# Four cross-attention layers on one core: the last wide job trades places with the first narrow job of layer 4

## What is computed

```
narrow (layers 0 and 3): xn = x * rsqrt(mean(x*x) + eps) * norm_w
    q = xn @ wq (16 heads of 8), k, v = cond @ wk, cond @ wv (4 key heads, shared by 4)
    x = x + softmax(q k^T / sqrt(8)) v @ wo
wide (layers 1 and 2): q = x @ Wq (16 heads of 64), k, v = ctx @ Wk, ctx @ Wv
    x = x + softmax(q k^T / 8 + col_bias) v @ Wo + bo
```

## Time and profile before

| | us |
|---|---|
| median of 3 runs | 382.94 |
| the runs | 382.94, 382.5, 452.04 |
| the profiled execution, its time | 384.65 |
| the profiled execution, its span | 382.9 |
| PE busy in the span | 359.0 |
| DVE busy | 268.5 |
| ACT busy | 278.9 |
| POOL busy | 187.4 |

### The profile page before, as it was taken

One profiled execution on the slowest core, in us unless ns is written; L12 is line 12 of the kernel. 1 busy time (PEld: TensorE's weight loads), 2 busy tenths in 40 slices (PEclk: granted clock), 3 DMA queues, 4 the chain that ended last, 5 costly groups with the idle time before them and its releaser, 6 DMA issues.

```text
span 382.9 us, 10493 instructions
## 1 busy us (share of the span) xinstructions
PE 359.0 (94%) x3522; PEld 319.2 (83%) x3522; DVE 268.5 (70%) x1401; ACT 278.9 (73%) x1176; POOL 187.4 (49%) x220
## 2 busy tenths in 40 slices
PE   6799899999999999999999999999999999978655
PEld 6698698899989998989889988888999889867444
DVE  0999985564654566696888886667465775699982
ACT  3687998875575585657798999997666865647891
POOL 1576964552332245446576765443333435447661
PEclk9789999999999999999999999999999999999998
DMA  7915000000000000000000000000000000000000
GB/s 229 409 57 221 0 3 3 2 3 0 3 2 2 1 2 3 2 1 2 3 9 9 7 10 2 3 3 2 0 3 2 3 2 1 2 3 3 7 7 15
DMA packets 4739, 9.91 MB, mean 26 GB/s; under 512 B 592, under 2 KB 3024, under 8 KB 4432
## 3 DMA queue, kind: packets, MB, share of 16 engines
q1 hardware_dynamic: 4400, 8.99, 6.7%
q10 hardware_dynamic: 288, 0.27, 0.2%
HBM read 8.73 MB, written 0.52 MB: 24 GB/s over the span
## 4 chain that ended last, share of the span: by engine, by line
PE 74%; DVE 17%; ACT 5%; DMA 1%; issue 1%; SPq 0%; DVEq 0%
PE pt_ps L844 12%; PE scores_ps L831 9%; PE v_ps L895 8%; PE fill_ps L696 8%; PE q_ps L791 8%; PE v_ps L877 7%; PE fill_ps L697 7%; PE fill_ps L698 7%; DVE probs L609 7%; ACT probs L478 4%; PE v_ps L865 3%; DVE probsT L620 3%; PE q_ps L783 3%; DVE qn L592 2%; PE scores_ps L820 2%; DVE qn L588 2%
## 5 line engine op out<-in xcount | busy, mean ns | idle before, releaser
L478 ACT ACTIVATE probs<-probs,negmax 128x128 f32<-128x128 f32 x512 | 198.6, 391 | 82.5 <-DVE negmax L609 82.4
L375 POOL TENSOR_TENSOR probs<-probs,inv 128x512 f32<-128x512 f32 x128 | 137.3, 1076 | 178.2 <-DVE inv L616 177.8
L478 ACT ACTIVATION_READ_ACCUMULATOR probs<-probs,negmax 128x1 f32 x512 | 97.0, 190 | 0.0
L609 DVE CUSTOM_DVE_ANT_0 probs<-scores_ps,col_bias 128x128 f32<-128x128 f32 x256 | 58.1, 283 | 39.1 <-PE scores_ps L831 39.1
L844 PE MATMUL pt_ps<-smalls,probs 128*128 128x128 f32 x512 | 69.2, 278 | 7.5 <-DVE probsT L620 7.5
L844 PEld LDWEIGHTS pt_ps<-smalls,probs 128*128 128x128 f32 x512 | 56.6, 142 | 19.1 <-issue 15.8
L609 DVE CUSTOM_DVE_ANT_0 probs<-scores_ps,no_bias,inv_rms 128x128 f32<-128x128 f32 x224 | 64.3, 344 | 6.1 <-PE scores_ps L820 5.7
L620 DVE COPY probsT<-pt_ps 128x512 f32<-128x512 f32 x96 | 62.9, 683 | 2.7 <-PE pt_ps L844 0.6
L609 DVE DVE_READ_ACCUMULATOR2_ANT negmax<- 128x1 f32 x512 | 42.5, 83 | 0.0
L696 PE MATMUL fill_ps<-c_hi,w_hi 128*128 128x256 f32 x128 | 38.5, 301 | 0.0
L831 PE MATMUL scores_ps<-kT,qT 64*128 64x128 f32 x512 | 37.2, 285 | 0.0
(11 more groups left out here) (92 smaller groups left out, 586.0 us busy)
## 6 DMA issues: line engine op xcount, KB each, us to landing
kT<-in_kv_w SPq DMA_DIRECT2D x6, 512.0 KB, 6.9
w_qo<-in_qo_w SPq DMA_DIRECT2D x2, 1024.0 KB, 8.6
v<-in_ctxT SPq DMA_DIRECT2D x4, 256.0 KB, 9.9
v<-in_kv_w SPq DMA_DIRECT2D x2, 512.0 KB, 11.7
outT<-x SPq DMA_DIRECT2D x8, 64.0 KB, 1.6
wn<-in_narrow_w SPq DMA_DIRECT2D x1, 384.0 KB, 6.0
x<-in_xT SPq DMA_DIRECT2D x1, 384.0 KB, 8.5
oT<-in_narrow_kv ACTq DMA_DIRECT2D x1, 256.0 KB, 2.8
```

The source lines that it names most:

```text
L375: nc.gpsimd.tensor_tensor(p4, p4, inv[:, o % 2, side, :].unsqueeze(2).broadcast_to([P, 4, S]), ALU.mult,).then_inc(probs_made[side], 1)
L478: last = nc.scalar.activation(e, e, ACT.Exp, scale=-1.0, bias=negmax[:, o % 2, side, q:q + 1], accum_out=rowsum[:, o % 2, side, q:q + 1])
L609: last = nc.vector.tensor_tensor_reduce(out=probs[:, o % PROBS_RING, side, cols], in0=banks[scores_bank(o)][side][:, cols], in1=bias, scal ...
```

## The change

Two entries of `JOBS` trade places: job 27 becomes (3, 4), narrow, and job 28 becomes (2, 7), wide. The order of the last six jobs is then wide, narrow, wide, narrow, narrow, narrow, where it was wide, wide and four narrow. Layer 3 of items 4 and 7 (jobs 27 and 31) now stands three jobs behind layer 2 of the same item, not four; `is_close` names these two. For them the queries and the mean of squares move to half 2n - 1 on PE, the split to 2n - 1 on DVE, the statistic to the head of half 2n on DVE, and on POOL `square` to 2n - 2 and `inverse_root` to 2n - 1, each between the two normalisations of that half. Three entries of `FILLS` move one or two halves back, and with them the half from which odd scores use `fill_ps` (59, was 57). Buffers of narrow jobs are picked by the index among narrow jobs in place of the parity of n, which gives the same numbers for jobs up to 26.

```diff
+FIRST_LAST, LAST_WIDE = JOBS.index((3, 4)), JOBS.index((2, 7))
+JOBS[FIRST_LAST], JOBS[LAST_WIDE] = JOBS[LAST_WIDE], JOBS[FIRST_LAST]
...
-    50: ["v7.0"], 52: ["v7.1"], 53: ["kn3.3"], 54: ["v7.2"], 55: ["v7.3"],
+    50: ["v7.0"], 52: ["v7.1"], 54: ["kn3.3"], 56: ["v7.2"], 57: ["v7.3"],
...
 def query_half(n):
 
+    if is_close(n):
+        return 2 * n - 1
     return 2 * n - 3 if n >= 2 and is_narrow(n - 1) else 2 * n - 2
 
+def split_half(n):
+
+    return 2 * n - 1 if is_close(n) else query_half(n) + 1
+
+def squares_half(n):
+
+    return 2 * n - 1 if is_close(n) else 2 * n - 2
+
+def is_close(n):
+
+    return is_narrow(n) and JOBS[n][0] > 0 and n - JOBS.index((JOBS[n][0] - 1, JOBS[n][1])) == 3
...
+def place(n):
+
+    return narrow_index(n) % 2
...
-                nc.gpsimd.tensor_tensor(inv_rms[:, n % 2:n % 2 + 1], rms[:, n % 2:n % 2 + 1], half_power[:],
+                nc.gpsimd.tensor_tensor(inv_rms[:, place(n):place(n) + 1], rms[:, place(n):place(n) + 1], half_power[:],
                                         ALU.pow).then_inc(rms_made, 1)
...
             def half(o):
                 if valid(o):
                     normalise(o, 0)
+                for n in NARROW_JOBS:
+                    if o == 2 * n - 2 and is_close(n):
+                        square(n)
+                    if o == 2 * n - 1 and is_close(n):
+                        inverse_root(n)
+                if valid(o):
                     normalise(o, 1)
                 for n in NARROW_JOBS:
-                    if o == 2 * n - 2 and n > 0:
+                    if o == 2 * n - 2 and n > 0 and not is_close(n):
                         inverse_root(n)
-                    if o == 2 * n - 4 and n >= 2:
+                    if o == 2 * n - 4 and n >= 2 and not is_close(n):
                         square(n)
...
-                if h == 1 and is_narrow(n + 1):
-                    mean_out(n + 1)
+                for m in NARROW_JOBS:
+                    if m > 0 and squares_half(m) == o - 1:
+                        mean_out(m)
...
-                    if m > 0 and query_half(m) == o - 1:
+                    if m > 0 and split_half(m) == o:
                         narrow_queries(m)
...
                 if n >= 3:
-                    pe.wait_ge(v_read, uses(n - 3, 1))
-                if n > 0 and is_narrow(n - 1):
-                    pe.wait_ge(rms_out, narrow_index(n - 1) + 1)
+                    pe.wait_ge(v_read, uses(n - 2, 0) if is_close(n) and is_wide(n - 2) else uses(n - 3, 1))
+                if n > 0:
+                    pe.wait_ge(rms_out, narrow_index(n))
...
-                if is_narrow((o + 4) // 2):
+                if is_narrow((o + 4) // 2) and squares_half((o + 4) // 2) < o + 3:
                     pe.wait_ge(rms_out, narrow_index((o + 4) // 2) + 1)
...
+                for m in NARROW_JOBS:
+                    if m > 0 and query_half(m) == o and is_close(m):
+                        queries(m, 0)
                 for name in FILLS.get(o, []):
                     project_context(name)
                 for m in NARROW_JOBS:
-                    if m > 0 and query_half(m) == o:
+                    if m > 0 and query_half(m) == o and not is_close(m):
                         queries(m, 0)
                 if is_wide(n + 1):
                     queries(n + 1, h)
-                if h == 0 and is_narrow(n + 1):
-                    mean_squares(n + 1)
+                for m in NARROW_JOBS:
+                    if m > 0 and squares_half(m) == o:
+                        mean_squares(m)
```

More of the change, by code:

```diff
@@ L349, in narrow_values @@
                     pool.wait_ge(v_full, uses(m, 1))
-                place = v_narrow[:, i % 2].rearrange("p (g s) -> p g s", g=KV_HEADS)[:, :, 0:NARROW_D]
+                blocks = v_narrow[:, i % 2].rearrange("p (g s) -> p g s", g=KV_HEADS)[:, :, 0:NARROW_D]
                 values = vn[:, b, NARROW.index(l)].rearrange("p (g d) -> p g d", g=KV_HEADS)
-                nc.gpsimd.tensor_copy(place, values).then_inc(vn_made, 1)
+                nc.gpsimd.tensor_copy(blocks, values).then_inc(vn_made, 1)
             def inverse_root(n):
                 pool.wait_ge(rms_out, narrow_index(n) + 1)
-                nc.gpsimd.tensor_tensor(inv_rms[:, n % 2:n % 2 + 1], rms[:, n % 2:n % 2 + 1], half_power[:],
+                nc.gpsimd.tensor_tensor(inv_rms[:, place(n):place(n) + 1], rms[:, place(n):place(n) + 1], half_power[:],
                                         ALU.pow).then_inc(rms_made, 1)
@@ L368, in square @@
                     pool.wait_ge(ms_full, narrow_index(n) - 1)
-                nc.gpsimd.tensor_tensor(x_sq[:, n % 2, :], x[:, b, :], x[:, b, :], ALU.mult).then_inc(sq_ready, 1)
+                nc.gpsimd.tensor_tensor(x_sq[:, place(n), :], x[:, b, :], x[:, b, :], ALU.mult).then_inc(sq_ready, 1)
             def normalise(o, side):
@@ L579, in mean_out @@
                 dve.wait_ge(ms_full, narrow_index(n) + 1)
-                nc.vector.tensor_scalar(rms[:, n % 2:n % 2 + 1], ms_ps[:, 0:1], EPS, None, ALU.add
+                nc.vector.tensor_scalar(rms[:, place(n):place(n) + 1], ms_ps[:, 0:1], EPS, None, ALU.add
                                         ).then_inc(rms_out, 1)
@@ L586, in narrow_queries @@
                 dve.wait_ge(q_full, uses(n, 0))
-                all_parts = qn[0:STACK, n % 2].rearrange("p r t -> p (r t)")
+                all_parts = qn[0:STACK, place(n)].rearrange("p r t -> p (r t)")
                 nc.vector.tensor_scalar(all_parts, q_ps[0:STACK, :], -NARROW_SCALE, None, ALU.mult).then_inc(qn_hi_made, 1)
@@ L590, in narrow_queries @@
                 low = slice(PART, 2 * PART)
-                rest = qn[low, n % 2].rearrange("p r t -> p (r t)")
+                rest = qn[low, place(n)].rearrange("p r t -> p (r t)")
                 nc.vector.scalar_tensor_tensor(
@@ L602, in scores_out @@
                 bias = no_bias[:].broadcast_to([P, S]) if l in NARROW else col_bias[:, l - 1, :]
-                scale = inv_rms[:, n % 2:n % 2 + 1] if l in NARROW else 1.0
+                scale = inv_rms[:, place(n):place(n) + 1] if l in NARROW else 1.0
                 if l in NARROW and h == 0 and side == 0:
@@ L798, in mean_squares @@
                 if n >= 3:
-                    pe.wait_ge(v_read, uses(n - 3, 1))
-                if n > 0 and is_narrow(n - 1):
-                    pe.wait_ge(rms_out, narrow_index(n - 1) + 1)
-                nc.tensor.matmul(ms_ps, x_sq[:, n % 2, :], mean_w[:, 0:2], start=True, stop=True).then_inc(ms_full, 1)
+                    pe.wait_ge(v_read, uses(n - 2, 0) if is_close(n) and is_wide(n - 2) else uses(n - 3, 1))
+                if n > 0:
+                    pe.wait_ge(rms_out, narrow_index(n))
+                nc.tensor.matmul(ms_ps, x_sq[:, place(n), :], mean_w[:, 0:2], start=True, stop=True).then_inc(ms_full, 1)
             def scores(n, h):
@@ L819, in scores @@
                     for side in range(2):
-                        nc.tensor.matmul(out[side][:], qn[0:STACK, n % 2, 2 * h + side, :], keys, start=True, stop=True
+                        nc.tensor.matmul(out[side][:], qn[0:STACK, place(n), 2 * h + side, :], keys, start=True, stop=True
                                          ).then_inc(scores_full[side], 1)
```

## The result

The changed kernel takes **389.5 us** (median of 4 runs, 387.75 to 391.06), the kernel before in the same series 382.72 (4 runs). The ratio is 1.0178, with a 95% interval of 1.0114 to 1.0241. One of the four runs before took 452.04 us, a slow one that the ratio leaves out. The median is 3.7 us above the forecast of 385.8 and just above the upper ends of both ranges given with it, 388.6 and 389.2. So it is slower, by 6.8 us in the first series and 4.3 in the second, where 2.9 were forecast.

A forecast was written before the change was run, and what follows sets the result against it. PE was busy 94% of the span, but DVE bound the tail from about 331.86 us. +3.8 us at scores 63, part given back, left +2.9: 382.9 + 2.9 = 385.8 us; own range 383.0 to 388.6, 8 in 10 380.6 to 389.2.

The forecast's parts named there:

- the mechanism of the schedule up to scores 63: Halves 52 to 62: new waits and gaps put DVE's scores 63 at 372.85 against 369.07, +3.8 us.
- DVE's idle time ahead of scores 54 and 62: Halves 54 and 62: DVE idle for some 1.7 us each, put down to the inverse root or its semaphore.
- the term of 1.8: Halves 54 and 62: reciprocal to scores through normalisation and inverse root on POOL, 0.25 + 1.0 + 0.55 us.
- The split wait on PE: Half 53: PE stands still ahead of scores 54 until DVE has split the narrow job's queries, about 1.5 us.
- the gap ahead of `add_input(26)`: Start of half 57: DVE idle 3.25 us, waiting for the output projection at the end of PE's half 56.
- the sum: Delay of DVE's scores 63 from all halves before it, forecast at +3.8 us.
- halves 52 to 54: Work taken off PE pays for both new waits; DVE's scores 55 come at 331.5 against 331.86, 0.35 us left.
- A part is given back: Drain: last transposes follow normalisation directly as the projection ahead ends sooner, cutting the +3.8 to +2.9 us.
- the same chain at the same clock: After the last transposes: the rest of the drain runs as before, so the sum stays +2.9 us.
- rival 2: Tail: standstills drop PE to 1.2 GHz by 360, before projection 28, adding 4.7 us: 390.5 us; chance 0.08.
- Rival 1: Halves 52, 53 and tail: narrow job fills DVE's 3.45 idle us; 380.8 us, at best 379.4; chance 0.22.

The follow-up runs named there:

- e5: Changed kernel with the close jobs' statistic and inverse root made earlier, plus unread constant matmuls in PE's tail standstills: 384.22 us, ratio 1.0011.
- e9: e5 with projection kn3.3 moved to half 53 and v7.2 to half 57, without the added matmuls of those halves: 382.74 us, ratio 0.9983.
- e8: Kernel before, with unread constant matmuls added in PE's standstills of halves 62, 64 and 66: 381.92 us, ratio 0.9952.
- e6: Changed kernel with unread constant matmuls added in PE's standstills from half 53 to 66: 387.34 us, ratio 1.0078.
- e7: Changed kernel, unaltered, measured again in a later series of 6 runs: 388.13 us, ratio 1.0114.
- e1: Changed kernel with the two close jobs' statistic made right behind the split and their inverse root ahead of both normalisations: 387.22 us, ratio 1.0067.
- e3: Kernel before, with unread constant matmuls added in halves 62 (5), 64 (8) and 66 (3): 382.6 us, ratio 0.9964.

## Why the prediction was wrong, step by step

- **Right: the mechanism of the schedule up to scores 63.** DVE's idle time ahead of scores 54 and 62 came at 1.62 and 1.63 us (forecast 1.7), and the term of 1.8, from the reciprocal to the scores, at 1.84 and 1.85. The split wait on PE was 1.47 (1.5), the gap ahead of `add_input(26)` 3.38 (3.25). At full clock the sum was 4.1 us for 3.8; most of the missing 0.3 is that halves 52 to 54 left 0.07 us and not 0.35. That the forecast has DVE's scores 63 at 372.85 and after at 372.70 is luck, since half 52 of after had started 1.05 us earlier. e5 and e9 shorten or remove these waits and get back 2.8 and 1.7 us, together about what the order costs.
- **Wrong: "A part is given back"** (0.9 us). Before, the last transposes came 2.20 us behind the last reciprocal. I read that as a fixed queueing behind the outputs of the job ahead, from which only the new order would be free. In e8, the old order with its drain at full clock, they come 1.34 us behind it (371.81 to 373.15 us): the delay was matmuls at 1.2 GHz. The new order is not free of that queue either: in e6, at full clock, it is 1.61 us (377.00 to 378.61), and the last transposes wait for DVE's copy `probsT`, which stands behind the copy of the values of job 30. In after it was 2.59. So nothing was given back: minus 0.9 became plus 0.5 at full clock (3.80 at scores 63, 4.28 at the last transposes, e6 against e8; 0.2 of the difference is there at the last reciprocal) and plus 0.6 in the recorded pair (4.7, 5.3).
- **Wrong: "the same chain at the same clock".** From last transposes to last output projection before took 3.85 us, after 5.16, e6 and e8 3.44 each. The recorded execution of after ran this at 1.2 GHz throughout. This is the clock of rival 2, but not its condition: I had priced only a fall before projection 28 that lasts, and given it 0.08. The clock did fall ahead of projection 28, at 353 us, but was back at 357, and projection 28 (360.65 us) and scores 61 and 62 ran at full clock. So that rival 2's 390.5 us lies close to the measured 389.5 is luck. The clock of the drain is also the part that varies: e7's execution took 3.66 us for the same rows.
- **The early dip.** At scores 63 after was at 4.7 us and not 3.8. 0.55 us of it is the dip around 355 us (the stretch to scores 62 is 59.13 us in after and 58.58 in e6), behind a standstill of 2.16 us. The rest is the 4.1 us of the schedule itself.
- **Rival 1, interleaving pays, fell.** Of the 0.35 us that halves 52 to 54 should have left, 0.07 came (DVE's scores 55 are 20.51 us behind scores 52, against 20.58 before), and nothing after it. The Trainium skill (Perfetto Trace Analysis, Optimization Strategy) says that interleaving regimes may help; no run here shows a gain. In e9, with the two waits for the inverse root gone and the gap ahead of `add_input(26)` down to 1.96 us, the new order is only even with the old one. Why it doesn't win by then, no run separates.
- **The size that stays open.** In the medians the clock costs both orders about the same: busy matmuls win 0.4% in after (1.0114 to 1.0078) and 0.5% in before (0.9952). By that the change should cost some 1.1 to 1.3%: 1.0114 for e7, and 1.0078 to 0.9952 for e6 against e8. The first series gave 1.8% from four runs with mean clocks of 0.972 to 0.982. The intervals overlap; whether its excess is more than the luck of four executions is not settled. Nor is how much the clock costs after on average: the rows have 3.2 us in one execution and 1.7 in another (e7, 73.77 us against 72.10), the medians 0.8. The intervals of these series reach 0.2 to 0.6% to either side, so that a change of 0.8% could well be told from none, other than the prediction has it.

By its own terms the forecast should have been 382.9 and 4.3 to 4.6, that is 387.2 to 387.5 us, with the clock moving single series by another 1 to 2 us, and a range to 391.

## What to carry to other kernels

Before a term is subtracted because "a queue will be shorter now", look at the granted clock over exactly those rows: a delay made of slow matmuls is no queue, and both orders can lose or regain it. Check fillers in the same way before a run with them is taken for one at full clock. Where the new order makes PE stand still several times near the end, as here for 1.5 to 2.5 us, give the forecast the drain at the lower clock as a case of its own. And when jobs are interleaved, count for each dependence how many jobs now lie between writer and reader: here three places instead of four turned a hidden statistic and inverse root into 1.6 us on the path, twice; moving one 0.16 us instruction and its inverse root forward took it off.

## What the runs showed of the hardware

- The clock in the half-busy tail differs from execution to execution of one program. Six executions of e7 have mean clocks of 0.967 to 0.982 and spans of 388.9 to 384.1 us, the longer ones at the lower clock. The 25 of the kernel before beside it had 0.969 to 0.996 and 384.7 to 379.3, with a looser tie: the one at 0.969 had 381.8.
- Every dip looked at followed a standstill or a stretch in which PE was half idle; that of after at 377 came behind 2.48 us of standstill and 1.19 us of transposes. That of e1 at 325 came behind two standstills of 1.47 and 0.91 us. With busy matmuls in these places the mean clock was 0.990 to 0.995 (e6), 0.987 to 1.000 (e8). The Trainium skill (TensorE: Matmul & The Clock Gate, What's actually happening) has the clock released by activity and otherwise gated; the traces agree, 0.50 behind standstills and 1.00 in e6 in the same places.
- Busy matmuls were free in these runs only where the clock was still up. Eight of them took 1.95 us in a standstill of e6 (half 64) and cost nothing there; in e3 five came too late, took 2.44 us at the lower level and stood in the way, as did six in e8, with 2.65 us.
